# Cross-attention and mixture of experts: the maxima of the softmax enter the second score product as two rows of the query diagonal

## What is computed

```python
Q = _split_heads(layernorm(x) @ Wq.T); K = _split_heads(ctx @ Wk.T); V = _split_heads(ctx @ Wv.T)
scores = jnp.einsum('bhqd,bhkd->bhqk', Q, K) / scale        # masked keys: -1e9
attn = jax.nn.softmax(scores, axis=-1)
x = x + jnp.einsum('bhqk,bhkd->bhqd', attn, V).transpose(0, 2, 1, 3).reshape(B, Lq, D_MODEL) @ Wo.T
x = x + ffn(layernorm(x))     # router softmax, top 2 of 8 experts, silu(x w1) * (x w3), then w2
```

## Time and profile before

| | us |
|---|---|
| median of three runs | 327.0 |
| profiled execution: its time | 327.09 |
| profiled execution: span of the trace | 325.3 |
| passes 1, 2, 3, from first second score to last first score | 49.0 to 72, 81.3 to 104, 112.9 to 141.7 |
| pass 4 | 142.3 to 202 |
| experts and output | 202 to 325.3 |

### The profile page before, as it was taken

The page is one execution under the profiler, slowest core; times in us unless marked ns, Lnnn a source line. Parts: engine busy times, 40 slices in busy tenths (PEclk is TensorE's granted clock), DMA queues, the critical chain, the costliest instruction groups (busy, mean ns, idle before and its releaser), DMA issues.

```text
span 325.3 us, 5807 instructions
## 1 busy us (share of the span) xinstructions
PE 233.3 (72%) x1591; PEld 180.4 (55%) x1591; DVE 219.9 (68%) x642; ACT 141.8 (44%) x318; POOL 114.3 (35%) x125
## 2 busy tenths in 40 slices
PE   0946788889898988747564818679674698899820
PEld 0733565667566656546342606658563697789710
DVE  5597965887598758857734424387862586688983
ACT  6792256546655664206321406335220354455400
POOL 5201250125011502033737360035277264555540
PEclk9986599999999999957977566799985699999975
DMA  6995504450443044510301154102113134428006
GB/s 177 256 260 105 123 2 87 83 115 11 90 91 81 2 97 99 134 61 2 82 24 53 34 111 97 27 8 61 50 51 70 33 82 94 106 51 217 26 11 194
DMA packets 43886, 27.31 MB, mean 84 GB/s; under 512 B 5030, under 2 KB 41397, under 8 KB 43856
## 3 DMA queue, kind: packets, MB, share of 16 engines
q1 hardware_dynamic: 40208, 20.95, 28.2%
q0 software_dynamic: 2816, 5.27, 5.4%
q10 hardware_dynamic: 832, 0.72, 0.8%
HBM read 13.27 MB, written 7.37 MB: 63 GB/s over the span
## 4 chain that ended last, share of the span: by engine, by line
PE 41%; DVE 20%; issue 9%; another core or an unknown queue 8%; SPq 7%; DMA 7%; ACT 5%; POOL 2%; POOLq 0%; DVEq 0%; ACTq 0%
PE bank L493 6%; SPq L421 6%; PE bank L499 4%; DVE m_neg L1356 4%; DMA bd<-st 3%; PE bank L649 3%; PE bank L731 3%; PE bank L652 2%; PE bank L666 2%; PE bank L732 2%; PE bank L705 2%; PE bank L718 2%; PE bank L627 2%; PE bank L708 2%
## 5 line engine op out<-in xcount | busy, mean ns | idle before, releaser
L1016 POOL DMA_INDIRECT ys<-big x46 | 45.3, 986 | 41.5 <-DVE big L1379 22.6
L1356 DVE TENSOR_REDUCE m_neg<-bank 128x4 f32<-128x512 f32 x64 | 43.4, 685 | 18.1 <-PE bank L666 17.8
L905 ACT ACTIVATE big<-bank 128x512 f32<-128x512 f32 x64 | 37.5, 597 | 25.6 <-PE bank L652 24.0
L774 ACT ACTIVATE st<-bank 128x128 fp32r<-128x128 f32 (+1 forms) x92 | 26.3, 329 | 35.0 <-PE bank L718 12.9
L731 PE MATMUL bank<-bd,st 128*128 x92 | 28.1, 327 | 10.5 <-DVE big L1379 10.1
L649 PE MATMUL bank<-m_bd,ones_b 128*128 128x512 f32 x64 | 31.7, 496 | 3.7 <-ACT big L905 1.9
L666 PE MATMUL bank<-bd,st 128*128 128x512 f32 x64 | 29.1, 477 | 7.2 <-DMA bd<-st 5.8
L968 POOL TENSOR_SCALAR ve<-mv 128x4 f32<-128x4 f32 x8 | 1.8, 228 | 87.0 <-DVE mv L1048 87.0
L1398 DVE TENSOR_TENSOR big<-big,bank 128x256 f32<-128x256 f32 x46 | 19.3, 419 | 16.2 <-ACT big L937 13.6
L1283 DVE SCALAR_TENSOR_TENSOR st<-st_hi,cst,bank 128x512 fp32r<-128x512 f32 x32 | 23.3, 747 | 8.8 <-ACT st_hi L774 4.3
L937 ACT ACTIVATE big<-bank 128x256 f32<-128x256 f32 x46 | 17.7, 385 | 25.9 <-PE bank L708 13.1
(11 more groups left out here) (172 smaller groups left out, 566.4 us busy)
## 6 DMA issues: line engine op xcount, KB each, us to landing
bd<-st SPq DMA_DIRECT2D x128, 64.0 KB, 2.1
big<-xg SPq DMA_DIRECT2D x46, 64.5 KB
raw<-ys SPq DMA_DIRECT2D x8, 256.0 KB, 3.2
xg<-in_patterns SPq DMA_DIRECT2D x18, 64.5 KB
x_all<-in_x SPq DMA_DIRECT2D x4, 256.0 KB, 4.3
rows<-in_mask_BxS_if POOLq DMA_DIRECT2D x4, 256.0 KB, 5.0
ctx_all<-in_L_ffn_w SPq DMA_DIRECT2D x1, 1024.0 KB, 5.9
out<-ctx_all SPq DMA_DIRECT2D x4, 256.0 KB, 3.8
```

The source lines that it names most:

```text
L774: return nc.scalar.activation(o, i, ACT.Copy)
L905: nc.scalar.activation(prob[n % 2][:, NJ * g:NJ * (g + 1), :].rearrange("p h q -> p (h q)"), s2[k % 2][:, :], ACT.Exp, scale=SCALE).then_i ...
L1016: pool.indirect_dma_start(ys[f], bass.IndirectOffsetOnAxis(xt[n % XR][:, D:RW].bitcast(I32), 0), y_sb[n % YR], None, bounds_check=2 * CAPS ...
L1356: nc.vector.tensor_reduce(m_neg[:, H * (b - 1) + NJ * g:H * (b - 1) + NJ * (g + 1)], s1[k % s1_ring(u)][:, :].rearrange("p (j q) -> p j q" ...
```

## The change

The constants lose C_HEAD and C_BATCH and gain C_MAX, a column with ones in rows 26 and 27 of each block of 32. The key stacks have ones in rows 26 and 27 (ACT adds C_MAX as a bias, where it copied before; DVE's multiplier C_CK keeps them). ones_b and m_bd are gone, and with them the product at line 649 and GpSimd's four multiplications. In their place GpSimd issues, for each batch, four direct DMAs that copy 8 rows of mT (high and low part of four groups of heads) into rows 26 and 27 of the query diagonal. DVE writes the maxima in another order (batch, head in the group, part, group), so that these 8 rows lie together. SP's copies of the query diagonal have 26 rows where they had 32. PE waits for the rows of a batch before its first second score.

```diff
-C_ID, C_CQ, C_CK, C_ONE, C_HEAD, C_BATCH, C_LOW, C_BIAS = 0, 128, 129, 130, 132, 148, 152, 216
+C_ID, C_CQ, C_CK, C_ONE, C_MAX, C_LOW, C_BIAS = 0, 128, 129, 130, 131, 152, 216
+MAX_ROW = 26
...
-    c[:, C_CK] = np.where((r >= 8) & (r < 16), -1.0, 0.0)
+    c[:, C_CK] = np.where((r >= 8) & (r < 16), -1.0, np.where((r == MAX_ROW) | (r == MAX_ROW + 1), 1.0, 0.0))
+    c[:, C_MAX] = (r == MAX_ROW) | (r == MAX_ROW + 1)
...
-                    rows = slice(R * j, R * (j + 1))
+                    rows = slice(R * j, R * (j + 1) if k else R * j + MAX_ROW)
...
                             if g == 0:
                                 diagonal_in(pe, 0, n)
+                                maxima_in(pe, n)
                             if k >= 2:
                                 pe.wait_ge(prob_ready, k - 1)
-                            if b == 0:
-                                pe.wait_ge(mbd_ready, NG * (u - 1) + g + 1)
-                            nc.tensor.matmul(s2[k % 2][:, :], ones_b[:, b, :],
-                                             m_bd[:, NJ * g:NJ * (g + 1), :].rearrange("p h q -> p (h q)"),
-                                             start=True, stop=False)
                             nc.tensor.matmul(s2[k % 2][:, :], st[:, (u - 1) % 2, 1, g, b * S:(b + 1) * S],
                                              bd_slot(0, n)[:, g, :, :].rearrange("p j q -> p (j q)"),
-                                             start=False, stop=True).then_inc(s2_full, 1)
+                                             start=True, stop=True).then_inc(s2_full, 1)
...
                         if is_k:
-                            i = copy(st_hi[:, n % SH, :], src)
+                            i = nc.scalar.activation(st_hi[:, n % SH, :], src, ACT.Identity, bias=cst[:, C_MAX:C_MAX + 1])
...
+            def maximum_rows(n):
+
+                u, b = divmod(n, QB)
+                taken(pool, ("MT", u))
+                if n >= 3:
+                    pool.wait_ge(s2_full, NG * (n - 2))
+                else:
+                    pool.wait_ge(bd_cleared, 6)
+                for j in range(NJ):
+                    row = R * j + MAX_ROW
+                    pool.dma_start(bd_slot(0, n)[row:row + 2, :, j, :].bitcast(F32),
+                                 mT[32 * b + 8 * j:32 * b + 8 * (j + 1), :].bitcast(F32)).then_inc(mrow_ready[n % 3], 16)
+
...
-                    taken(pool, ("MT", u - 1))
-                    if u >= 2:
-                        pool.wait_ge(s2_full, NG * QB * (u - 1))
-                    for g in range(NG):
-                        nc.gpsimd.tensor_tensor(m_bd[:, NJ * g:NJ * (g + 1), :], mT[:, :].unsqueeze(1).to_broadcast([P, NJ, P]),
-                                                cst[:, C_HEAD + NJ * g:C_HEAD + NJ * (g + 1)].unsqueeze(2).to_broadcast([P, NJ, P]),
-                                                ALU.mult).then_inc(mbd_ready, 1)
+                    for b in range(QB):
+                        maximum_rows(QB * (u - 1) + b)
...
-            nc.vector.tensor_copy(ones_b[:, :, :], cst[:, C_BATCH:C_BATCH + QB].unsqueeze(2).to_broadcast([P, QB, P])
-                                  ).then_inc(setup_ready, 1)
...
-                nc.vector.tensor_copy(m_hl[:, 0, :], m_hi[:, :].bitcast(F32))
-                nc.vector.tensor_tensor(m_hl[:, 1, :], m_neg[:, :], m_hi[:, :].bitcast(F32), ALU.subtract).then_inc(mhl_ready, 1)
+                by_row = m_hl[:, :, :].rearrange("p a m -> p (a m)").rearrange("p (b j a g) -> p b j a g", b=QB, j=NJ, a=2)
+                by_head = [m[:, :].rearrange("p (b g j) -> p b j g", b=QB, g=NG) for m in (m_hi.bitcast(F32), m_neg)]
+                nc.vector.tensor_copy(by_row[:, :, :, 0, :], by_head[0])
+                nc.vector.tensor_tensor(by_row[:, :, :, 1, :], by_head[1], by_head[0], ALU.subtract).then_inc(mhl_ready, 1)
```

More of the change, by code:

```diff
@@ L91, in constants @@
     c[:, C_CQ] = np.where((r >= 16) & (r < 24), -1.0, np.where((r == 24) | (r == 25), 1.0, 0.0))
-    c[:, C_CK] = np.where((r >= 8) & (r < 16), -1.0, 0.0)
+    c[:, C_CK] = np.where((r >= 8) & (r < 16), -1.0, np.where((r == MAX_ROW) | (r == MAX_ROW + 1), 1.0, 0.0))
+    c[:, C_MAX] = (r == MAX_ROW) | (r == MAX_ROW + 1)
     c[:, C_ONE] = (r == 24) | (r == 25)
-    for h in range(H):
-        c[:, C_HEAD + h] = p % H == h
-    for b in range(QB):
-        c[:, C_BATCH + b] = (p // H) % QB == b
     for e in range(E):
@@ L212, in program @@
         bias_w = sb("bias_w", [P, P], F32R)
-        ones_b = sb("ones_b", [P, QB, P], F32R)
         stats = sb("stats", [P, QB, 6])
@@ L230, in program @@
         m_hl = sb("m_hl", [P, 2, QB * H])
-        mT = sb("mT", [P, P])
-        m_bd = sb("m_bd", [P, H, P], F32R)
+        mT = sb("mT", [P, P], F32R)
         unused = sb("unused", [P, 1])
@@ L345, in program @@
         mhl_ready = sem("mhl_ready")
-        mbd_ready = sem("mbd_ready")
+        mrow_ready = [sem(f"mrow_ready{k}") for k in range(3)]
         s2_full, prob_ready = sem("s2_full"), sem("prob_ready")
@@ L376, in diagonal_in, with maxima_in @@
             engine.wait_ge((kbd_ready if k else qbd_ready)[n % 3], 16 * NJ * (n // 3 + 1))
+        def maxima_in(engine, n):
+            engine.wait_ge(mrow_ready[n % 3], 16 * NJ * (n // 3 + 1))
         x_d = x.rearrange("(u b) s d -> u s b d", b=QB)
@@ L1114, in _ @@
             nc.vector.tensor_copy(stack_columns(ws_lo), three_times(w_lo)).then_inc(ws_ready, 1)
-            nc.vector.tensor_copy(bias_w[:, :], cst[:, C_BIAS:C_BIAS + P])
-            nc.vector.tensor_copy(ones_b[:, :, :], cst[:, C_BATCH:C_BATCH + QB].unsqueeze(2).to_broadcast([P, QB, P])
-                                  ).then_inc(setup_ready, 1)
+            nc.vector.tensor_copy(bias_w[:, :], cst[:, C_BIAS:C_BIAS + P]).then_inc(setup_ready, 1)
             def take_projection(n):
@@ L1254, in _ @@
                     if u >= 2:
-                        dve.wait_ge(mbd_ready, NG * (u - 1))
+                        for n in range(QB * (u - 1) - 3, QB * (u - 1)):
+                            maxima_in(dve, n)
                     nc.vector.tensor_copy(mT[:, :], work_bank(("MT", u - 1))[:, 0:P]).then_inc(into_sbuf(("MT", u - 1)), 1)
```

## The result

The changed kernel takes 334.03 us (median of 4 runs, 332.06 to 334.99) where the kernel before takes 326.99 us: a ratio of 1.019, 95% interval 1.013 to 1.026. It is 7.0 us slower; the forecast was 1.7 us slower. The profiled execution took 334.99 us, with a span of 333.2 us for 325.3 before.

What follows compares the result with a forecast made beforehand. PE was taken to bound passes 1 to 3, with DVE and SP's issues close, and the start of GpSimd's sends to set pass 4's end. Sum -2.6 + 0.3 + 4.6 - 0.6 = +1.7 us: 328.8 us, range 323.5 to 339.

Steps and rivals of the forecast that it cites:

- rival C: Passes 1 to 3: TensorE's clock falls in step 1, some 2 us a pass, 335 us; chance 0.10.
- rival A: GpSimd's row DMAs cost more than 0.73 us each: 332 us at 1.0, 347 at 1.31; chance 0.20.
- Pass 4, +4.6 less 0.6: Pass 4: row DMAs and deviation delay GpSimd's first send by 4.7 us, taken as 4.6 lost, 0.6 back.
- The 0.6 that I gave back behind the gaps: Pass 4: PE's saving not hidden by the gaps, one product at 197.16 and its neighbour wait, 0.6 us.
- the unnamed gaps: Pass 4: three PE gaps of 3.04, 7.61 and 9.01 us, no awaited thing named, taken to end after sends.
- Passes 1 to 3, -2.6 + 0.3: Passes 1 to 3: removed products save 2.6 us of 11, and the key stacks' bias adds 0.3 us.
- step 0's products: Step 0 of a pass: removing 12 products, 2.8 us, saves nothing, since the keys' diagonal landing ends the step.
- p = 0.73: GpSimd: the distance of two row DMAs, assumed 0.73 us, between 0.6 and 1.31.
- Landing 2.2: Row DMAs of 4 KB land after 2.2 us, so PE waits for nothing; at 5.0, 1 us a pass.
- The bias of 0.3: Passes 1 to 3: ACT's key stack copy with bias shows 0.09 us once a pass, 0.3 in three.
- Rival B: Pass 4: the gaps don't hang on GpSimd and absorb the delay, PE keeps its savings: 322.6 us; chance 0.13.
- Rival D: Passes 1 to 3: GpSimd's row DMAs hold up PE's value products, about 3 us a pass, 338 us; chance 0.05.

Runs made afterwards that it cites:

- e5: The kernel before, with GpSimd's first send held back until the sixth second score of pass 4: 308.85 us, ratio 1.018.
- e8: The changed kernel with pass 4's row DMAs issued by SyncE (SP) with semaphores of their own, passes 1 to 3 untouched: 304.45 us, ratio 1.000.
- e2_sends_first: The changed kernel with pass 4's last four row DMAs behind the first eight sends: 304.41 us, ratio 1.001; run again on another chip, 304.84 us, 1.004.
- e4: e2_sends_first with each second score of step 0 of passes 1 to 3 computed four times: 304.79 us, ratio 1.002.
- e9: e8 with each second score of step 0 of passes 1 to 3 computed four times: 301.63 us, ratio 0.989.
- e7: e2_sends_first with every second score of passes 1 to 3 computed twice, in all four steps: 306.37 us, ratio 1.006.
- b0_before: The kernel before, unchanged, run once more on another chip: 305.15 us, ratio 1.003.

## Why the prediction was right or wrong

The time, 334.03 us, lies in the range, but not in the forecast's own (326 to 331.5): the mechanism of pass 4 was right, and one term of the sum was lost to rival C. That the range held is in part luck. Its upper end came mostly from A, which didn't happen; and of the 6.2 us by which the spans differ more than the forecast's 1.7, passes 1 to 3 are 3.6 and pass 4 is 0.2, while 2.4 lie in the start and the experts, which I had put at nothing. C's 335 is near the measured time for that reason too.

- **Pass 4, +4.6 less 0.6: right.** mT to ys is 4.2 us longer. The first send is 5.2 us later for 4.7 forecast, by errors that nearly cancel. The twelve and the four row DMAs were quicker (0.55 us each for 0.73), so the twelve were out 7.2 us behind mT for 9.1 (152.0 less 142.9) and the four took 2.17 us for 2.9. The last four started 11.9 us behind mT for 10.6, because the 1.5 us that I had given to the missing products ahead of the fourth second score didn't come. PE in the changed kernel, then in the kernel before:

```profile
153.35 1.06 PE L499 MATMUL bank<-cst,raw 128*128 128x128 f32 x4
...
155.48 0.48 PE L648 MATMUL bank<-bd,st 128*128 128x512 f32 x1
```

```profile
152.58 0.60 PE L499 MATMUL bank<-cst,raw 128*128 128x128 f32 x4
...
154.60 0.39 PE L652 MATMUL bank<-bd,st 128*128 128x512 f32 x1
```

  The same four transposes take 1.06 us for 0.60. The fourth second score stands 10.8 us behind mT for 11.7, 0.9 us earlier and not 1.5, and the row DMA starts 0.66 us after that product's end, a distance that I had left out. The 0.6 that I gave back behind the gaps shows nowhere by itself. Placing the start of the sends as what sets the end of pass 4 was right, and e5 and e8 show it from both sides: late sends alone cost 4.9 us up to ys, and sends on time give pass 4's loss back. The reason that I gave, the unnamed gaps, isn't needed for it: on chips without gaps the last send's landing and the gather from xg are what the experts wait for. What the gaps of the first chip are stays open. They move with the sends in both kernels there; none of the experiments ran on that chip, so a kernel with other sends wasn't tried against them.
- **Passes 1 to 3, -2.6 + 0.3: wrong, and the step that failed is the one that gave step 0's products the price nothing.** They were 2.8 us of work in time that PE spends waiting for ACT and a DMA, and I read "hidden" as "free to take away". But they had helped to keep the clock up: with them gone the clock fell behind step 0 of pass 2 in all seven traces, and that step 1 took 5.3 us on the first chip for 3.61. This was rival C, with a chance of 0.10; I held against it that the stacks just ahead are dense, which didn't help. I had it in every pass, 2 us each; behind step 0 it comes always in pass 2, in four of seven traces in pass 3 and in one (e2_sends_first) in pass 1, and one stretch of 3.4 us costs a pass about 1 us, since the next step makes up for some of it. On the first chip, with three such stretches (one of them behind the wait for the queries' diagonal), passes 1 to 3 lost 3.1 us (102.2 against e4's 99.1, on another chip); between e8 and e9 it is 1.8. The other half of the term was right: with the clock up the three passes take 99.1 and 99.2 us, 1.7 to 1.8 us under the 100.9 of the first trace, where I had -2.3. But the kernel before takes 100.8 to 102.1 us there by itself, so a loss of 1.3 us between two single traces would be no finding without the place of the low stretches. The Trainium skill, TensorE: Matmul & The Clock Gate (Part 1: The HAM clock gate), says that the gate follows how busy the array has been; the runs agree in direction: with step 0 of pass 2 busy for 4.20 us of 4.46 (e9), the clock stayed up, with 2.08 of 4.43 (e8) it fell.
- **p = 0.73: too high, and rival A didn't happen.** The row DMAs stand 0.55 us apart, under even the lower end that I had set (0.6, SP's issue). Bounding from above by the indirect sends (1.31) gave the range much of its upper part, and they were another kind of instruction.
- **Landing 2.2: 1.7 us.** No wait of PE ends on bd<-mT in the trace of the changed kernel or in e7's. (GpSimd's first multiplication of pass 1 began at 42.37, not at 42.2; nothing hangs on it.)
- **The bias of 0.3: right.** From mT to the first second score pass 2 takes 7.56 us for 7.43 before, and pass 3 7.55 for 7.43: 0.1 a pass, as forecast. In pass 1 it doesn't show (7.07 for 7.06).
- **Rival B (the gaps absorb the delay): no.** They moved with the sends. **Rival D: no,** e7 has the row DMAs and the passes of the kernel before.
- **The experts, +1.9:** not forecast. This stretch has the same code in all kernels, and takes 98.0 to 101.6 us in the twelve traces of the other chips, b0_before's 100.0 among them (107.9 and 109.9 on the first chip); so 1.9 us are of the size of what it varies by itself, and the cause wasn't looked for. Nor was that of the 0.5 us at the start.

## What to carry over

A product that hides in PE's idle time may still hold up PE's clock: before taking PE's work out of a thin stretch, look at what runs right behind it at full load, and price that at half the clock. And before a low clock is put down to a change, see where it lies: of the seven traces here with a low clock in pass 1, five have it from a stretch that began in pass 0. A cheap DMA on a queue costs not its own duration but the wait that it brings along: here four DMAs of 0.55 us held sends that wait for nothing of theirs, because they themselves waited for a score; give such work a queue that has nothing urgent behind it (e8), or put it behind. And where two effects of one change oppose each other, undo each alone: e8 came out level and looked like the end of it, and only with the clock mended as well (e9) was the change faster. e4, which differs from e9 in who issues pass 4's row DMAs, was level, so that gain wants a second measurement.

## What the runs showed of the hardware

- Small direct DMAs on GpSimd (4 KB, inside SBUF) are issued every 0.55 us and land in 1.7 us; the indirect ones beside them every 1.28 to 1.34 us. SP issues the same 4 KB more slowly: twelve took 8.12 us in e8, 0.68 each.
- The granted clock isn't the same in two executions of one kernel: e2's pass 1 had 0.94 and 1.00 on two chips, pass 2 0.89 and 0.95. A comparison of two spans without the clock beside them would have put this down to the code.
- A product computed four times over in place of once cost nothing where PE would have waited, and with it no low stretch stood behind step 0: passes 2 and 3 were 1.8 us shorter together (e8 and e9).
- A stretch of 3.4 us at 1.2 GHz cost a pass about 1 us: pass 3 took 38.0 to 38.2 us with it and 36.7 to 37.0 without, in the same code.
- The kernel before takes 327 us on the first chip and 304 to 305 us on three others. Of the difference 15.9 us lie in pass 4, where the first chip's unnamed gaps stand (from mT to ys 74.5 us against 58.6), and some 8 in the experts (107.9 against 100.0); why isn't known.
